# AdaLN block with attention and a mixture of low-rank experts: Strassen's scheme for the output projection of 14 groups, with the keys' rotation on VectorE ahead of the sums of the first token pair

## The chip, the cores and the metric

One core of a Trainium2 chip runs the kernel. The metric is the device time of one execution in microseconds; the time before is 2559.74 us, the median of 3 runs (2558.72 to 2560.05).

## The reference

Four batches of 512 tokens, width 1024. The part that matters here:

```
h = _layernorm(x) * (1 + ca) + sa
q = (h @ wq), k = (h @ wk), v = (h @ wv)      # 32 query heads, 8 key/value heads, 128 wide
q = _rope(q, pos); k = _rope(k, pos)
scores = q k^T * HEAD_DIM ** (-0.5)           # window of 256 keys, causal
out = softmax(scores) v                       # (tokens, 4096)
x = x + ga * (out @ wo)                       # wo is 4096 x 1024
```

An expert stage follows, which the change leaves as it is. Everything is float32.

## The kernel before

**Numbers.** Each matmul operand is split into a high and a low part (`float32r`), and `mm3` (L787) makes one product of three matmuls (lines L788 to L790). ScalarE (ACT) or GpSimd (POOL) copies the high part, VectorE (DVE) or GpSimd subtracts the low one.

**Groups.** The work is 32 groups, `n = 8 * batch + g`, one for each batch and key/value head: four query heads, one key head, one value head, and the 512 x 1024 share of the output projection that belongs to the four heads. In batch 0 the split weights are made and stored; from batch 1 on SyncE (SP) fetches them.

**One group on TensorE (PE).** `pe_attention` goes through 16 units `u` (token tile `u // 4`, head `u % 4`): scores of unit `u + 3` (L841), the turn of unit `u`'s probabilities (L859, matmul line L864), one chunk of the next group's keys in the first eight, and after every fourth unit the values of a token tile (L867). The output projection is eight halves (token tile, 512 columns) of 12 matmuls each (`pe_wo`, L816); four halves lie between the units 8 to 15 and four behind the attention. The next group's four query heads of 24 matmuls follow (`pe_project`), then its values (`pe_v`).

**Around it.** `dve_wo` (L1261) adds each half from PSUM to `acc`. `act_rope` (L1026) and `dve_rope` (L1233) rotate the keys (r = 0) and the query heads (r = 1 to 4): ScalarE copies the swapped halves, VectorE multiplies and adds, ScalarE copies the high part, VectorE subtracts the low part. `pool_group` (L766) makes the difference of the values `vd` and, for the units 8 to 15 (folded, two token tiles), multiplies a part of `pT` (L783). The values of a folded tile end with matmuls on `vd` that need these.

**SyncE's queue** runs strictly in the program's order. In a group it fetches the query and value weights when the old ones are used (`sp_fetch_qv`, L538), the keys' weights and, once the group before has projected its output, `w_o` (`sp_fetch_ko`, L545). In the first four groups of the batches 1 and 2 it also stores the next batch's normalised tile, `sp_tile_store` (L528); the tile's buffers share memory with `pT`, so ScalarE waits for this store (`s_hst`, end of `act_project`, L1082) before it goes on to the next attention. Between batches `sp_reload` (L570) loads the next batch's `hT`, which the last attention of the batch needs for its keys' chunks.

Of the kernel before, what the change touches and what calls it, by code (L numbers as in the profile page):

```python
# [19 lines left out]
F32 = mybir.dt.float32  # L20
# [34 lines left out]

def key_tiles(i):

    return list(range(max(0, i - WINDOW // P), i + 1))
# [32 lines left out]
def adaln_block(nc, x, x_turned, wq, wk, wv, wo, gate_wT, lora_aT, lora_bT, c, wmod, cos, sin, mask, keep, lower, ident, iota, out):  # L91
# [8 lines left out]
    ln_d = nc.dram_tensor("ln_scratch", (P, 2), F32, kind="Internal").ap()  # L100
    hT_d = [nc.dram_tensor(f"hT_{z}_scratch", (BATCH * P, KT, SEQ), F32, kind="Internal").ap() for z in ("hi", "lo")]

    with ExitStack() as top:
# [226 lines left out]
        def p0_pe(eng):  # L330
# [23 lines left out]
            pe_v(eng, 0, False)  # L354
# [14 lines left out]
        w_o = split_pair(p1, "w_o", [P, GQ, D])  # L369
        qo = split_pair(p1, "qo", [P, GQ, SEQ])  # L370
# [26 lines left out]
        prob = sb(p1, "prob", [P, GQ, 3 * P])  # L397
# [19 lines left out]
        with ExitStack() as a:  # L417
            lx = sb(a, "lx", [P, D])
            lf = sb(a, "lf", [P, KT, P])
            l_hi, l_lo = split_pair(a, "l", [P, KT, P])  # L420
            r_hi, r_lo = split_pair(a, "r", [P, KT, P])
        p1.close()
# [34 lines left out]
        s_dq = [sem(f"s_dq{c}") for c in range(KT // 2)]  # L457

# [74 lines left out]
        def sp_direct_group(eng, n, before_o=None):  # L533

            sp_fetch_qv(eng, n)
            sp_fetch_ko(eng, n, before_o)
# [8 lines left out]
        def sp_fetch_ko(eng, n, before_o=None):  # L545

            eng.wait_ge(s_proj, 6 * n + 2)
            if isinstance(n, int) and n == GROUPS - 1:
                eng.wait_ge(s_mm1, KT * 3)
                sp_last_rows(eng, 0)  # L550
            else:
                sp_fetch(eng, 5, (n + 1) % KV, s_dk)
            if before_o:
                before_o()
            eng.wait_ge(s_wo, 8 * n + 1)
            for j in range(6, NC):
                sp_fetch(eng, j, n % KV, s_do)
# [43 lines left out]

        def sp_groups(eng, b, rows, store):
            for t in range(QT):
                n = b * KV + 1 + t
                if not store:
                    sp_lora_load(eng, t)
                    sp_direct_group(eng, n, lambda: sp_tile_load(eng, n, rows(t)))
                else:
                    sp_turned_load(eng, b, t)
                    sp_direct_group(eng, n, lambda: sp_turned_row(eng, b, t))  # L610
                if store:
                    sp_tile_store(eng, b, t)
                else:
                    sp_lora_keep(eng, t)
            if store:
                with eng.Fori(1 + QT, KV) as g:
                    sp_direct_group(eng, b * KV + g)
            else:
                for g in range(1 + QT, KV):
                    n = b * KV + g  # L620
                    q = g - QT
                    sp_direct_group(eng, n, (lambda: sp_part(eng, q, n)) if q < 3 else None)
                    if q == 1:
                        sp_store_gate(eng, 1, part_row)
# [21 lines left out]
        def p1_sp(eng):  # L646
# [24 lines left out]
            sp_fetch_ko(eng, KV)  # L671
            for b in range(1, last):
                sp_groups(eng, b, lambda t: x_tile(b, t), True)
                sp_reload(eng, b + 1)
                sp_direct_group(eng, (b + 1) * KV)
# [75 lines left out]
        def p1_pool(eng):  # L751
# [8 lines left out]
            for b in range(1, BATCH):  # L760
                eng.wait_ge(s_fin, 2 * QT * b)
                plain(eng.memset(acc[:], 0.0)).then_inc(s_acc0, 1)
                with eng.Fori(0, KV) as g:
                    pool_group(eng, b * KV + g)

        def pool_group(eng, n):  # L766
# [6 lines left out]
            eng.wait_ge(s_fold, FOLD_STEPS * n + 2)  # L773
            eng.tensor_tensor(far[:, 0], far[:, 0], far[:, 1], ALU.add).then_inc(s_fold, 1)
            eng.wait_ge(s_fold, FOLD_STEPS * n + 3)
            plain(eng.tensor_copy(vd[:, 0], far[:, 0])).then_inc(s_fold, 1)
            eng.wait_ge(s_fold, FOLD_STEPS * n + 4)
            eng.tensor_tensor(vd[:, 1], far[:, 0], vd[:, 0].bitcast(F32), ALU.subtract).then_inc(s_fold, 1)
            for u in range(UNITS - FOLDED, UNITS):
                i, h = divmod(u, GQ)  # L780
                pair = pT_all[i % 2][:, :, :, h * P:(h + 1) * P]
                eng.wait_ge(s_ptl, UNITS * n + u + 1)
                eng.tensor_tensor(pair[:, :, 2, :], pair[:, :, 0, :].bitcast(F32), lower_t[:].unsqueeze(1).broadcast_to([P, 2, P]),  # L783
                                  ALU.mult).then_inc(s_fold, 1)
# [31 lines left out]
        def pe_wo(eng, n, half, direct):  # L816

            t, c = divmod(half, 2)
            if half == 0:
                if direct:  # L820
                    eng.wait_ge(s_do, 128 * (n - (KV - 1)))
# [4 lines left out]
            if 1 <= half < FILL:  # L826
                eng.wait_ge(s_wor, 8 * n + half + 1)
            elif half >= FILL + 3:
                eng.wait_ge(s_wor, 8 * n + half - 1)
# [9 lines left out]
        FOLD_STEPS = VD_STEPS + FOLDED  # L839
# [27 lines left out]
        def pe_values(eng, n, i):  # L867
            eng.wait_ge(s_ptl, UNITS * n + GQ * (i + 1))
            if i == 0:
                eng.wait_ge(s_v, n + 2)  # L870
            else:
                eng.wait_ge(s_ol, QT * n + i)
            kts = key_tiles(i)
            for b, kt in enumerate(kts[:prob_tiles(i)]):
                m = mm3(eng, OBANK[:], sl(v_, lambda v: v[:, kt, :]), sl(pT[i % 2], lambda p: p[:, b, :]), b == 0, b == len(kts) - 1)
            if folded(i):
                z = i - WINDOW // P
                eng.wait_ge(s_fold, FOLD_STEPS * n + VD_STEPS + GQ * (z + 1))
# [9 lines left out]
        def pe_attention(eng, n, k_at, k_direct, b1=None, o_direct=True, late=False):  # L888
            for u in range(UNITS):
# [31 lines left out]
                if u % GQ == 1 and u > GQ:  # L921
                    pe_values(eng, n, u // GQ - 1)
                if u in WO_AT:
                    pe_wo(eng, n, WO_AT.index(u), o_direct)
            pe_values(eng, n, QT - 1)
# [7 lines left out]
        def pe_qv(eng, n, direct, tile=None, part=None):  # L933
            for h in range(GQ):
                def between(k):
# [1141 lines left out]
```

## Time and profile before

| | |
|---|---|
| median of 3 runs | 2559.74 us |
| the profiled execution | 2558.81 us, span 2556.8 us |
| TensorE busy | 2532.4 us, 99% of the span |
| VectorE, ScalarE, GpSimd busy | 1609.7, 1112.4, 460.2 us |
| the 16 DMA engines | 52.5% (SyncE's queue), 197 GB/s |
| the chain that ended last | 95% on TensorE |

Busy time tells how long an engine had an instruction in it; matmuls overlap, so their starts tell the pace. The chain names the engine that the end waited for.

### The profile page before, as it was taken

What the parts mean: (1) busy time and instruction counts of PE and PEld (TensorE: products, weight loads), DVE (VectorE), ACT (ScalarE), POOL (GpSimd) and SP (SyncE); (2) the same over time, 40 slices, a digit from 0 to 9 for tenths busy, and PEclk for the clock granted to TensorE, in tenths of its full rate; (3) what the DMA queues carried; (4) which work ended last, traced back from release to release, by engine and by line L of the source; (5) the groups of instructions that cost most, each with busy time, mean ns of one, the idle gap of its engine ahead of it and who ended that gap; (6) DMA issues with size and microseconds to landing.
All of it is one profiled execution on the core that took longest, in us unless ns stands there. A gap on an engine that the chain in (4) does not pass through costs nothing.

```text
span 2556.8 us, 40925 instructions
## 1 busy us (share of the span) xinstructions
PE 2532.4 (99%) x12449; PEld 2101.0 (82%) x12449; DVE 1609.7 (63%) x4594; ACT 1112.4 (44%) x2585; POOL 460.2 (18%) x498
## 2 busy tenths in 40 slices
PE   7999999999999999999999999999999999999999
PEld 4888888887888888888888888888888888887887
DVE  6677776666666665556666665556666665556553
ACT  4555654443445443333445543333333443335441
POOL 0332233332111111102111110111111110101122
PEclk9999999999999999999999999999999999999999
DMA  8766676659445554347444554347554556446221
GB/s 339 280 222 241 246 271 224 244 179 374 171 158 190 199 183 151 117 149 298 167 167 166 197 183 164 137 148 267 189 204 175 203 201 228 180 170 261 101 83 58
DMA packets 160949, 504.15 MB, mean 197 GB/s; under 512 B 17552, under 2 KB 43984, under 8 KB 159312
## 3 DMA queue, kind: packets, MB, share of 16 engines
q1 hardware_dynamic: 156384, 486.65, 52.5%
q10 hardware_dynamic: 4464, 16.25, 1.7%
q8 instruction: 51, 0.84, 0.1%
q14 instruction: 50, 0.41, 0.0%
HBM read 381.17 MB, written 121.68 MB: 197 GB/s over the span
## 4 chain that ended last, share of the span: by engine, by line
PE 95%; DVE 2%; ACT 1%; DMA 1%; issue 1%; DVEq 0%; POOL 0%; ACTq 0%; SPq 0%; POOLq 0%
PE bank L788 30%; PE bank L790 29%; PE bank L789 29%; PE bank L864 4%; PE bank L853 1%; PE bank L1904 1%; PE bank L276 1%; PE bank L905 0%; DMA x1s<-x_scratch 0%; PE bank L303 0%; DMA wm<-in_wmod 0%; ACT w_o_hi L715 0%; PE bank L854 0%; PE bank L1955 0%; DVE qo_lo L1270 0%
## 5 line engine op out<-in xcount | busy, mean ns | idle before, releaser
L788 PE MATMUL bank<-w_o_hi,qo_hi 128*128 128x512 f32 x1024 | 411.4, 402 | 2.0 <-DVE qo_lo L1270 1.5
L790 PE MATMUL bank<-w_o_hi,qo_lo 128*128 128x512 f32 x1024 | 400.4, 391 | 0.0
L788 PE MATMUL bank<-hT_hi,w_q_hi 128*128 128x512 f32 x1024 | 399.5, 390 | 0.2 <-DVE swapped L1242 0.2
L789 PE MATMUL bank<-w_o_lo,qo_hi 128*128 128x512 f32 x1024 | 398.9, 390 | 0.0
L789 PE MATMUL bank<-hT_lo,w_q_hi 128*128 128x512 f32 x1024 | 398.5, 389 | 0.0
L790 PE MATMUL bank<-hT_hi,w_q_lo 128*128 128x512 f32 x1024 | 398.5, 389 | 0.0
L1050 ACT ACTIVATE prob<-prob,nbias 128x256 f32<-128x256 f32 (+1 forms) x512 | 247.3, 483 | 237.8 <-DVE nbias L1289 230.9
L783 POOL TENSOR_TENSOR pT<-pT,lower_t 128x256 fp32r<-128x256 f32 x256 | 196.0, 766 | 475.3 <-DVE pT L1323 475.3
L1241 DVE TENSOR_TENSOR rotated<-bank,cos_t 128x512 f32<-128x512 f32 x160 | 110.6, 692 | 261.8 <-ACT swapped L1035 261.1
L1265 DVE TENSOR_TENSOR acc<-bank,acc 128x512 f32<-128x512 f32 x256 | 173.7, 689 | 160.9 <-PE bank L790 160.8
L772 POOL TENSOR_TENSOR rotated<-v_all 128x256 f32<-128x256 f32 x64 | 48.1, 773 | 1231.5 <-DVE v_all L1329 1231.5
L1034 ACT ACTIVATE swapped<-bank 64x512 f32<-64x512 f32 x160 | 95.4, 596 | 360.4 <-PE bank L790 353.0
L1323 DVE TENSOR_TENSOR pT<-bank,pT 128x256 fp32r<-128x256 f32 (+1 forms) x512 | 195.7, 382 | 85.5 <-ACT pT L1147 85.3
L1147 ACT ACTIVATE pT<-bank 128x256 fp32r<-128x256 f32 (+1 forms) x512 | 177.5, 353 | 155.2 <-PE bank L864 150.2
L790 PEld LDWEIGHTS bank<-w_o_hi,qo_lo 128*128 128x128 f32 x1024 | 192.2, 188 | 42.2
L788 PEld LDWEIGHTS bank<-hT_hi,w_q_hi 128*128 128x128 f32 x1024 | 192.2, 188 | 42.0 <-issue 1.6
L788 PEld LDWEIGHTS bank<-w_o_hi,qo_hi 128*128 128x128 f32 x1024 | 192.3, 188 | 40.1 <-issue 3.2
L790 PEld LDWEIGHTS bank<-hT_hi,w_q_lo 128*128 128x128 f32 x1024 | 192.2, 188 | 40.0
L789 PEld LDWEIGHTS bank<-hT_lo,w_q_hi 128*128 128x128 f32 x1024 | 192.3, 188 | 39.6
L789 PEld LDWEIGHTS bank<-w_o_lo,qo_hi 128*128 128x128 f32 x1024 | 192.8, 188 | 36.7
L1289 DVE CUSTOM_DVE_ANT_0 prob<-bank,mask_t 128x256 f32<-128x256 f32 x384 | 162.4, 423 | 32.8 <-PE bank L864 10.9
L864 PE MATMUL bank<-ident_t,prob 128*128 128x128 f32 x896 | 177.1, 272 | 2.6 <-DVE prob L1299 2.1
(258 smaller groups left out, 4975.4 us busy)
## 6 DMA issues: line engine op xcount, KB each, us to landing
w_q_hi<-w_q_hi_scratch SPq DMA_DIRECT2D x96, 512.0 KB, 8.3
w_q_lo<-w_q_lo_scratch SPq DMA_DIRECT2D x96, 512.0 KB, 8.9
w_o_hi<-w_o_hi_scratch SPq DMA_DIRECT2D x96, 512.0 KB, 7.8
w_o_lo<-w_o_lo_scratch SPq DMA_DIRECT2D x96, 512.0 KB, 8.5
stage<-in_wq SPq DMA_DIRECT2D x32, 512.0 KB, 4.5
stage<-in_wo SPq DMA_DIRECT2D x32, 512.0 KB, 5.3
w_q_hi_scratch<-w_q_hi SPq DMA_DIRECT2D x32, 512.0 KB, 6.3
w_q_lo_scratch<-w_q_lo SPq DMA_DIRECT2D x32, 512.0 KB, 7.2
```

The source lines that it names most:

```text
L783: eng.tensor_tensor(pair[:, :, 2, :], pair[:, :, 0, :].bitcast(F32), lower_t[:].unsqueeze(1).broadcast_to([P, 2, P]), ALU.mult).then_inc(s ...
L788: eng.matmul(o, st[0], mv_[0], start=start, stop=False)
L789: eng.matmul(o, st[0], mv_[1], start=False, stop=False)
L790: return eng.matmul(o, st[1], mv_[0], start=False, stop=stop)
L864: m = eng.transpose(bank[5 + u % 2][:, b * P:(b + 1) * P], prob[:, u % GQ, b * P:(b + 1) * P], ident_t[:])
L1034: eng.activation(swapped[slot][0:half, :], bk[half:HD, :], ACT.Copy)
L1050: eng.activation(tile, tile, ACT.Exp, bias=nbias[:, u:u + 1], scale=-1.0, accum_out=rowsum[:, u:u + 1]).then_inc(s_exp, 1)
L1147: eng.activation(pT[i % 2][0][:, 0:nk, h * P:(h + 1) * P], bank[5 + u % 2][:, 0:nk * P].rearrange("p (b q) -> p b q", q=P), ACT.Copy).then ...
L1241: eng.tensor_tensor(rotated[slot][:], bk[:], cos_t[:], ALU.mult).then_inc(s_dve, 1)
L1265: eng.tensor_tensor(a, wo_bank(half)[:], a, ALU.add).then_inc(s_wor, 1)
L1289: plain(eng.tensor_tensor_reduce(prob[:, u % GQ, 0:w], SBANK[u % 3][:, 0:w], add, -SCALE, FAR, ALU.add, ALU.min, nbias[:, u:u + 1])).then_ ...
L1323: eng.tensor_tensor(lo, bank[5 + u % 2][:, 0:nk * P].rearrange("p (b q) -> p b q", q=P), hi.bitcast(F32), ALU.subtract).then_inc(s_ptl, 1)
```

## The change

In the batches 2 and 3 (`PAIRED = 2`) the groups but the last of each batch, 14 in all, project their output in two pairs of token tiles, (0, 1) and (2, 3). For a pair the blocks are two token tiles by two halves of the heads, times two halves of the heads by two halves of the columns, and seven products take the place of eight: `pe_product` is 6 matmuls, a pair 42, a group 84 where it had 96. The order is `ORDER = (3, 4, 1, 5, 2, 7, 6)`.

- **TensorE** runs all products behind the attention, two of them ahead of the last tile's values; the chunks of the next group's first query head take the halves' places between the units 8 to 15.
- **GpSimd** makes the five sums of attention outputs a pair (`pool_sum`) and their low parts (`pool_low`), 20 operations of 128x256 a group. The sums 1, 7 and 6 of the second pair go into the first pair's buffers and wait for its products 1, 7 and 6.
- **ScalarE** copies each tile's outputs whole (`flat_o`), the high half of them that is used plain, and the ten high parts of the sums (`act_highs`). Three of these stand between the swapped copies of the keys and their high part.
- **VectorE** adds or subtracts each product into one or two blocks of `acc`, 24 operations a group for 8 (`dve_product`), and rotates the keys after the first four.
- **The mixed weights** (five combinations of `wo` blocks a group) are made in batch 1 by GpSimd, four pieces a group for 7 groups, 28 in all, through one buffer, and stored to DRAM by SyncE: three pieces after each of the first four groups' folds, four after the others'.
- **SyncE** fetches weights one head and one product at a time in the paired groups.

```diff
+        def pool_mix(eng, piece):
+            (b11, b12), (b21, b22) = ((r[:, 0, :], r[:, 1, :]) for r in raw)
+            lo = mix_lo[:].bitcast(F32)
+            eng.wait_ge(s_raw, WS_KEPT + 32 * piece + 32)
+            eng.wait_ge(s_mixd, WS_KEPT + 32 * piece)
+            eng.tensor_tensor(lo[:, 0, :], b11, b22, ALU.add)
...
+            plain(eng.tensor_copy(mix_hi[:], lo)).then_inc(s_mix, 1)
...
+            eng.tensor_tensor(mix_lo[:], lo, mix_hi[:].bitcast(F32), ALU.subtract).then_inc(s_mix, 1)
+        def sp_mix_step(eng, at, piece, following):
+            eng.wait_ge(s_mix, 3 * at + 1)
+            if following is not None:
+                sp_mix_load(eng, following)
+            eng.wait_ge(s_mix, 3 * at + 3)
+            sp_mix_store(eng, piece)
...
+                    sp_direct_group(eng, n, b, lambda: sp_turned_row(eng, b, t))
+                    sp_mix(eng, 3 * t, [piece(3 * t + i) for i in range(4)])
+                    sp_tile_store(eng, b, t)
+                with eng.Fori(1 + QT, KV) as g:
+                    sp_direct_group(eng, b * KV + g, b)
+                    sp_mix(eng, 4 * g - 8, [piece(i, g - 2) for i in range(5)])
...
+        def pool_sum(eng, n, b, p, i):
...
+            if p == 1 and i in (1, 7, 6):
+                eng.wait_ge(s_wo, wo_at(n, b) + 1 + ORDER.index(i) + 1)
+            eng.tensor_tensor(mixed_sum(p, i)[2], x, y, op).then_inc(s_fold, 1)
...
+        M_FREE = ({7: 2, 6: 4}, {4: 6, 1: 8, 5: 10, 2: 11, 7: 12, 6: 14})
+        def pe_product(eng, n, b, p, i):
...
+            if i in M_FREE[p]:
+                eng.wait_ge(s_wor, wor_at(n, b) + 1 + M_FREE[p][i])
...
-            act_rope(eng, n, 0, False)
+            act_rope(eng, n, 0, False, (lambda: act_highs(eng, n - 1, b, ((1, 1), (1, 7), (1, 6)))) if b is not None else lambda: None)
...
         def act_groups(eng, b, ln):
+            if b == PAIRED:
+                eng.wait_ge(s_mixd, WS_KEPT + 32 * PIECES * (KV - 1))
...
+        def dve_paired_group(eng, n, b, part=None, turned=None, g=None):
+            dve_attention(eng, n - 1, b, tile=turned, paired=True)
...
+            dve_rope(eng, n, 0)
+            for i in ORDER[2:]:
+                dve_product(eng, n - 1, b, 0, i)
+            for i in ORDER:
+                dve_product(eng, n - 1, b, 1, i)
```

SyncE in a group of the first four of batch 1, from the last fetch of `w_o` on (`raw` holds the blocks of `wo`, `mix` the combinations, `l` the tile for the next batch):

```order
L569 DMA w_o_lo<-w_o_lo_scratch 128x1024
L756 DMA raw<-in_wo 128x2x256 [waits s_mix]
L756 DMA raw<-in_wo 128x2x256
L764 DMA w_s_hi_scratch<-mix_hi 640x1x256 [waits s_mix]
L764 DMA w_s_lo_scratch<-mix_lo 640x1x256
...
L592 DMA hT_hi_scratch<-l_hi 1024x1x128 [waits s_llo]
```

Before, the store of the tile followed the fetch of `w_o` directly; now three mixing steps, each like the one shown, stand between. Behind the loop of batch 1's last groups, which ends with four such steps, comes the reload of `hT`.

ScalarE at the end of a paired group's attention, up to the keys' high part:

```order
L1519 ACTIVATE flat_o<-bank 128x512 [waits s_pv]
L1520 ACTIVATE qo_hi<-bank 128x2x128
L1511 REGISTER_ALU
L1512 ACTIVATE qo_hi<-qo_sum 128x2x128 [waits s_fold]
L1403 ISA
L1408 ACTIVATE swapped<-bank 64x512 [waits s_proj]
L1409 ACTIVATE swapped<-bank 64x512
L1511 REGISTER_ALU
L1512 ACTIVATE sums_o_hi<-sums_f 128x256 [waits s_fold]
...
L1420 ACTIVATE kt_all<-rotated 128x512 [waits s_ra]
```

Three copies of `sums_o_hi` (one is shown) now lie between the swapped copies and the keys' high part; before, nothing did.

VectorE at the same place:

```order
L1650 TENSOR_TENSOR rotated<-rotated,swapped 128x512 [waits s_dve,s_rs]
L1662 TENSOR_TENSOR kt_all<-rotated,kt_all 128x512 [waits s_ra,s_rh]
L1680 REGISTER_ALU
L1684 ISA [waits s_wo]
L1686 TENSOR_TENSOR acc<-acc,bank 128x512 [waits s_wor]
```

The keys' low part, which waits for ScalarE's high part (`s_rh`), stands ahead of the 20 sums that remain; before, it stood ahead of four.

## Rows read from the trace of the kernel before

**Rows 1.** The page: busy time by engine, and the chain that ended last.
```profile
PE 2532.4 (99%) x12449; PEld 2101.0 (82%) x12449; DVE 1609.7 (63%) x4594; ACT 1112.4 (44%) x2585; POOL 460.2 (18%) x498
PE 95%; DVE 2%; ACT 1%; DMA 1%; issue 1%; DVEq 0%; POOL 0%; ACTq 0%; SPq 0%; POOLq 0%
```

**Rows 2.** TensorE's timeline, one group's last four halves: start us, us.
```profile
1323.09 0.39 PE L788 MATMUL bank<-w_o_hi,qo_hi 128*128 128x512 f32 x1
...
1333.97 0.39 PE L788 MATMUL bank<-hT_hi,w_q_hi 128*128 128x512 f32 x1
```

**Rows 3.** Groups of instructions by line: busy us, mean ns, idle before.
```profile
L783 POOL TENSOR_TENSOR pT<-pT,lower_t 128x256 fp32r<-128x256 f32 x256 | 196.0, 766 | 475.3 <-DVE pT L1323 475.3
L720 POOL TENSOR_TENSOR w_q_lo<-stage,w_q_hi 128x1024 fp32r<-128x1024 f32 x28 | 66.7, 2400 | 23.8 <-ACT w_q_hi L715 23.8
L776 POOL CAST vd<-rotated 128x256 fp32r<-128x256 f32 x32 | 12.7, 397 | 4.2
L762 POOL MEMSET acc<- 128x4096 f32 x3 | 10.6, 3529 | 79.5 <-DVE xb L1540 79.5
L1147 ACT ACTIVATE pT<-bank 128x256 fp32r<-128x256 f32 x384 | 142.6, 380 | 149.3 <-PE bank L864 144.4
L1044 ACT ACTIVATE qo_hi<-rotated 128x512 fp32r<-128x512 f32 x128 | 80.9, 632 | 210.8 <-DVE rotated L1245 210.8
L1265 DVE TENSOR_TENSOR acc<-bank,acc 128x512 f32<-128x512 f32 x256 | 173.7, 689 | 160.9 <-PE bank L790 160.8
L1257 DVE TENSOR_TENSOR qo_lo<-rotated,qo_hi 128x512 fp32r<-128x512 f32 x128 | 88.3, 690 | 55.9 <-ACT qo_hi L1044 55.9
L1434 DVE TENSOR_TENSOR stage<-stage 128x1024 f32<-128x1024 f32 x8 | 9.8, 1226 | 8.5 <-DMA stage<-ln_scratch 8.5
```

**Rows 4.** SyncE's DMA issues in batch 1, group 10: start us, us.
```profile
763.91 0.33 SPq L508 DMA_DIRECT2D w_o_hi<-w_o_hi_scratch  x1
...
767.60 0.47 SPq L508 DMA_DIRECT2D w_o_lo<-w_o_lo_scratch  x1
782.66 0.53 SPq L531 DMA_DIRECT2D hT_hi_scratch<-l_hi  x1
```

**Rows 5.** DMA of the first 20 us of that stretch, GB/s in 0.5 us slices.
```profile
GB/s 0 0 0 49 164 172 270 188 344 254 238 262 320 426 410 377 393 393 434 410 410 426 426 426 410 418 418 295 57 0 0 0 0 0 0 0 0 0 0 0
```

**Rows 6.** DMA issues of the whole run: KB each, us to landing.
```profile
hT_lo_scratch<-l_lo SPq DMA_DIRECT2D x12, 512.0 KB, 5.6
lora_b_lo_scratch<-l_lo SPq DMA_DIRECT2D x2, 512.0 KB, 3.6
```

**Rows 7.** ScalarE and TensorE where attention of that group starts.
```profile
790.54 0.40 ACT L1050 ACTIVATE prob<-prob,nbias 128x128 f32<-128x128 f32 x1 [0.47 <-DVE nbias L1289]
794.26 0.27 PE L864 MATMUL bank<-ident_t,prob 128*128 128x128 f32 x1
```

**Rows 8.** TensorE: first matmul on the folded values, attention of group 17.
```profile
1317.15 0.39 PE L788 MATMUL bank<-pT,vd 128*128 128x512 f32 x1
```

**Rows 9.** SyncE and TensorE: output weights of groups 15 and 17, keys of 16.
```profile
1119.16 0.33 SPq L508 DMA_DIRECT2D w_o_hi<-w_o_hi_scratch  x1
1152.24 0.48 PE L788 MATMUL bank<-hT_hi,w_k_hi 128*128 128x512 f32 x1
1263.11 0.33 SPq L508 DMA_DIRECT2D w_o_hi<-w_o_hi_scratch  x1
```

**Rows 10.** End of batch 1: GpSimd's last fold, SyncE's fetch, ScalarE's third exponential.
```profile
1177.60 0.73 POOL L783 TENSOR_TENSOR pT<-pT,lower_t 128x256 fp32r<-128x256 f32 x1 [0.19 <-DVE pT L1323]
1192.06 0.33 SPq L508 DMA_DIRECT2D w_o_hi<-w_o_hi_scratch  x1
1218.69 0.40 ACT L1050 ACTIVATE prob<-prob,nbias 128x128 f32<-128x128 f32 x1 [0.72 <-DVE nbias L1289]
```

**Rows 11.** GpSimd and VectorE in batch 0, two inputs from SBUF each.
```profile
121.69 2.40 POOL L720 TENSOR_TENSOR w_k_lo<-stage,w_k_hi 128x1024 fp32r<-128x1024 f32 x1 [1.61 <-ACT w_k_hi L715]
123.47 1.17 DVE L1242 TENSOR_TENSOR swapped<-swapped,sin_t 128x512 f32<-128x512 f32 x1
```

More of the change, by code:

```diff
@@ new lines, in sp_mix_load, with sp_mix_store @@
+        def sp_mix_load(eng, piece):
+            g, jc = (piece[0], piece[1])
+            j, half = divmod(jc, 2)
+            for y in range(2):
+                rows = wo[bass.ds(g * GQ * HD + (j + 2 * y) * HD, HD), :].rearrange("p (c s n) -> p c s n", c=2, s=2)[:, :, half, :]
+                eng.dma_start(raw[y][:], rows).then_inc(s_raw, 16)
+        def sp_mix_store(eng, piece):
+            g, jc = piece
+            j, half = divmod(jc, 2)
+            for z, tile in enumerate((mix_hi, mix_lo)):
+                to = w_s[z][bass.ds(g * P, P), :].rearrange("p (i j s n) -> p i j s n", i=len(MIXED), j=2, s=2)[:, :, j, half, :]
+                eng.dma_start(to, tile[:].bitcast(F32)).then_inc(s_mixd, 16)
@@ L611, in sp_groups @@
[L611 to L624, printed above, removed]
+                    sp_paired_group(eng, n, b, False, lambda: sp_tile_load(eng, n, rows(t)), lambda: sp_lora_keep(eng, t))
@@ L626, in x_tile @@
+            for g in range(1 + QT, KV):
+                n = b * KV + g
+                q = g - QT
+                sp_paired_group(eng, n, b, g == KV - 1, (lambda: sp_part(eng, q, n)) if not store and q < 3 else lambda: None)
+                if not store and q == 1:
+                    sp_store_gate(eng, 1, part_row)
         def x_tile(b, t):
@@ L759, in p1_pool @@
             pool_group(eng, KV - 1)
-            for b in range(1, BATCH):
+            eng.wait_ge(s_fin, 2 * QT)
+            plain(eng.memset(acc[:], 0.0)).then_inc(s_acc0, 1)
+            with eng.Fori(1, 1 + QT) as g:
+                pool_group(eng, KV + g - 1)
+                for i in range(3):
+                    pool_mix(eng, 3 * g - 3 + i)
+            with eng.Fori(1 + QT, KV + 1) as g:
+                pool_group(eng, KV + g - 1)
+                for i in range(4):
+                    pool_mix(eng, 4 * g - 8 + i)
@@ L1023, in adaln_block, with pe_group, act_rope @@
+        def pe_group(eng, n, b, direct, tile=None):
+            pe_attention(eng, n - 1, b, K_AT, direct, o_direct=direct)
+            for half in range(FILL, 8):
+                pe_wo(eng, n - 1, b, half, direct)
+            pe_qv(eng, n, direct, b, tile)
         OUT_STEP = {GQ * i + GQ + 1 + LAG: i for i in range(QT - 1)}
-        def act_rope(eng, n, r, split, between=lambda: None):
+        def act_rope(eng, n, r, split, between=lambda: None, b=None):
             slot = r % 2
```

584 lines of the change are left out of this document (452 added, 132 removed).

## The prediction

> **What bounds the kernel now.** I read the page first: TensorE has an instruction in it for 99% of the span, and 95% of the chain that ended last lies on it [rows 1]. So a matmul removed is time removed, as long as no new wait takes its place, and a wait put before TensorE costs its full length. The pace comes from the timeline: the 48 matmuls of four halves take 1333.97 - 1323.09 = 10.88 us, 0.227 us each [rows 2]. The next views tell what lies beside TensorE: GpSimd is the idlest engine (18%) but slow per element [rows 3], SyncE's queue runs in order [rows 4], and ScalarE's first work of an attention stands close behind the tile's store [rows 7].
>
> **The change, part by part.** The sum is made against the profiled execution, 2558.8 us, 0.9 us below the median of the runs.
>
> *Fewer matmuls.* 12 of 96 go in each of 14 groups: 12 x 0.227 = 2.7 us a group, **-38 us**. The first query head's chunks between the units cost what they cost behind the attention.
>
> *The keys' rotation ahead of the sums.* On VectorE the keys' low part waits for ScalarE's high part; that copy now stands behind three copies of sums, the last of which needs GpSimd's sum 6 of the second pair, and this one needs TensorE's product 6 of the first pair to be done. TensorE meanwhile has one product to run, the second pair's 3 (6 x 0.227 = 1.4 us); the next, 4, needs the bank of product 1, which VectorE has left standing behind the keys. The chain: end of the matmul behind its successor's start 0.16 (0.39 less 0.227) [rows 2], GpSimd's sum 0.77, ScalarE's copies 0.38 and 0.63, VectorE's low part 0.69, two sums, 0.6 and 0.69 [rows 3], six handings-over at some 0.06 (an estimate): 4.3 us. Less 1.4 that is 2.9 us a group. GpSimd can still hold it: in batch 0 a VectorE operation with two SBUF inputs took 1.17 us and ended 0.55 us after GpSimd's, where its median is 0.68 [rows 11]. The keys' low part is such an operation and GpSimd then makes low parts. I add 0.4: 3.3 us x 14 = **+46 us**. Bounds: 2.5 (the three engines overlap more) to 4 us (GpSimd half an operation late twice), 35 to 56 us. The Trainium skill, "SBUF — State Buffer", section on the two separate sides, says that VectorE with two SBUF inputs and GpSimd share one port pair and the loser is fully blocked; the rows agree. By that rule the wait is 3.3 us, without it 2.9, some 6 us over 14 groups.
>
> *VectorE's 16 further sums* are 16 x 0.6 = 9.6 us a group. They end some 3 us behind the last product, and one query head of 24 matmuls (5.4 us) covers this in a plain group. In the four groups of batch 2 that also normalise a tile, two operations of 1.23 us [rows 3] and ScalarE's eight pieces follow in the same chain, and TensorE waits for a bank: 1.8 us at the last head and about 1 at the first turn, 2.9 us x 4 = 12, and about 1 us in each of the four groups that split the experts' weights: **+16 us**, bounds 0 and 30.
>
> *The pieces of mixed weights in batch 1.* A piece on GpSimd is five sums of 256 columns (5 x 0.75), a cast of 1280 and a subtraction of 1280. 1024 columns of subtraction took 2.40 us, so 3.0; a cast of 256 took 0.40 and 4096 columns of memset 3.5, so about 1.3 [rows 3]. Together 8.1 us. One buffer holds it, so the next piece waits for the store, 1.31 MB in two DMAs. Pairs of 0.52 MB took 5.6 + 0.6 us (runs of 512 bytes) and 3.6 + 0.4 us (4 KB) from the first issue to the last landing [rows 6]; with 2 us fixed and the rest in proportion that is 4.5 to 7.3, and I take 6, since the runs are 1 KB. A piece's cycle is then 14.3 us with 0.2 of waits.
>
> - *Groups 9 to 12, three pieces.* Take group 10, where the fetch of `w_o` is issued at 763.9 [rows 4]. GpSimd made its first piece long before, but SyncE can only now store it: issued at 769, behind 4.2 MB that occupy the engines to about 777 [rows 5]; 0.52 MB of `raw` and the store land at 782. Second piece to 790.2, landed 796.4, third to 804.6. Only then does SyncE issue the store of the tile, at 782.7 before [rows 4]: with 2.4 MB in line, landed at 814.5. ScalarE waits for this store before the attention; its third exponential ran at 790.5, TensorE's turn of that unit at 794.3 [rows 7]. From the release to the turn are 1.7 us of work: 816.3. That is 22 us, four times: **+88 us**. Low end: no line behind `w_o` and the shortest stores, tile landed at 801, 8.4 us; high end 26 us; 34 to 104.
> - *Attentions 13 and 14, four pieces.* Counted from the fetch of `w_o`, the fourth piece ends at 18.1 + 8.1 + 2 x 14.3 + 0.2 = 55 us. Then the values' difference (3.7, five operations) and four folds (3.1) are still to do: 62 us. TensorE wanted them at 1317.15 - 1263.11 = 54.0 [rows 8, 9]. **+16 us** for both, 0 to 28.
> - *Attention 15.* SyncE reloads `hT` only behind the fourth piece's store: 1119.2 + 55 = 1174.2, first pair landed 8.9 us later (2 fixed, 4.1 for the store, 2.6 for 1.05 MB at 410 GB/s, 0.2). The keys' chunk that needs it ran at 1152.2 [rows 9]. **+31 us**, 19 to 36.
> - *Attention 16.* ScalarE waits for all 28 stores. GpSimd is free at 1178.3 [rows 10]; the pieces end at 1187, 1202, 1218 and 1232, the second and third also held by the weights fetched from 1192.1 on [rows 10]; the last store has 4.2 MB ahead, landed 1240.6. The exponential ran at 1218.7 [rows 10]; after the same correction of 2 us **+20 us**, 8 to 25.
>
> Batch 1 gives 88 + 16 + 31 + 20 = 155 us, the paired groups -38 + 46 + 16 = +24. The sum is 2558.8 + 179 = **2738 us**, slower. With all low ends it is 2617, with all high ends 2800.
>
> **What stays free.** The weights' fetches of the paired groups have most of a group each (71 us) to land, and the DMA engines are little over half used. The sums on GpSimd in the attention: 16 operations of 0.8 us lie between the values' low part and the last fold, some 17 us with the waits, against a need on TensorE about 20 us after it; if they were 3 us slower, the last tile's values would wait. VectorE in the attention loses four sums to `acc` and gains nothing; its steps of about 1.4 us lie under TensorE's.
>
> **The rivals.**
> 1. *Some of batch 1 is hidden.* The stores land earlier than the order of issue says and a piece is quicker. With all four at their low ends and the rest as summed: 2558.8 + 24 + 61 = 2644. For it: 410 GB/s are reached in the queue [rows 5]. Against: two pieces alone are 16 us, and the tile's store had only 1.2 us of room between its landing (issue of the second DMA some 0.6 us behind 782.66, and 5.6: 788.8) and ScalarE's wait.
> 2. *The mixing costs nothing.* The paired groups alone decide: 2583, slower still. It would take the tile's store issued by 784, two pieces and two stores within 20 us of the fetch of `w_o`: not possible with pieces of 8 us [rows 3].
> 3. *Faster: TensorE's shorter run shows.* Mechanism: GpSimd finishes its pieces before anyone asks, and the keys' chain is covered by the second pair's product 3. Place: TensorE between products 3 and 4. It decides once that chain falls under 1.4 us and the waits of batch 1 under 38 us together; the price is -38: 2521. Against it: five operations of known length stand in the chain.
> 4. *GpSimd and VectorE block each other in batch 1 too.* Subtractions of 3.0 us hold rotations, and these hold pieces. The pieces then take 10 us: 2 us more in each of the 2 to 3 pieces that stand in each of the waits, some 16 + 12 + 6 + 6 = 40 us: 2778, and up to 2800.
>
> That the change does not do what it says can be left out: the order shows 84 matmuls for 96 in the paired groups.
>
> **How the numbers follow.** The sum as it stands (2680 to 2765) has 0.58; rival 4 (2765 to 2800) 0.13; rival 1 (2600 to 2680) 0.14; rival 2 (2562 to 2600) 0.07; faster 0.06; no change 0.02. The range 2635 to 2785 takes the first whole, most of rival 4 and most of rival 1, about 0.8. A difference of 0.2% (5 us) is about what a measurement of this kernel can tell from none. Faster 0.06, same 0.02, slower 0.92.
>
> **What would show it.** In the profile after: ScalarE idle for about 22 us before an exponential or a copy of `pT`, released by the DMA into the scratch of `hT`, four times; TensorE idle about 31 us before the keys' chunk of attention 15, released by a load of `hT`; 14 waits of 2.5 to 4 us before the second pair's product 4, released by VectorE's sums; pieces about 14 us apart on GpSimd. The prediction is wrong if the tile's store lands before ScalarE asks for it, if pieces follow each other in 9 us, or if TensorE goes from product 3 to 4 without a wait.

## The result, and the profile after

The changed kernel takes 2813.47 us (median of 4 runs, 2810.20 to 2816.11) against 2559.45 us before in the same comparison: 1.099 times the time, 95% interval 1.097 to 1.101. That is slower by 254 us, where 2738 us and 179 us were forecast, and above the range's end of 2785 us.

The page of the changed kernel, the rows that answer to [rows 1], and the granted clock of TensorE in 40 slices of the span (tenths of full speed, all 9 before):

```profile
PE 2555.4 (91%) x12281; PEld 2097.1 (75%) x12281; DVE 1817.4 (65%) x4818; ACT 1166.0 (41%) x2781; POOL 892.4 (32%) x974
PEclk9999999999889889997989999999999999999999
PE 63%; issue 11%; POOL 8%; DMA 7%; DVE 6%; ACT 3%; SPq 2%; DVEq 0%; POOLq 0%; ACTq 0%
```

TensorE's busy time is 23 us longer although it has 168 matmuls fewer, since some of them ran at half the clock, and it now stands idle for 9% of the span. GpSimd's busy time has nearly doubled (460.2 to 892.4 us). The chain that ended last lies on TensorE for 63% where it was 95%; GpSimd and DMA, which hardly stood in it before, have 15% together, and 11% is "issue", time in which nothing that the profile shows was waited for.

The view of waits, TensorE's rows (us in total, times, longest):

```profile
PE bank L1243 <- DVE prob L1727: 143.6, 29, 26.3
PE bank L1079 <- DVE acc L1686: 38.2, 14, 3.0
PE bank L1079 <- DMA hT_lo<-hT_lo_scratch: 29.9, 1, 29.9
PE bank L1079 <- DVE acc L1670: 9.3, 8, 1.9
PE bank L1079 <- POOL pT L1074: 8.6, 2, 4.3
```

The second row is the forecast chain of the keys. The first mixes four waits of 18.5 to 18.8 us for the tile's store, one of 26.3 at the entry into batch 2, and smaller ones. The last is the wait for GpSimd's folds in attentions 13 and 14.

TensorE's timeline, the first matmul of each group's values, of the changed kernel, groups 9 to 17 but for 12 (start us, us); between two such rows lies the first one's attention:

```profile
716.49 0.45 PE L1079 MATMUL bank<-hT_hi,w_v_hi 128*128 128x512 f32 x1
815.34 0.45 PE L1079 MATMUL bank<-hT_hi,w_v_hi 128*128 128x512 f32 x1
914.04 0.45 PE L1079 MATMUL bank<-hT_hi,w_v_hi 128*128 128x512 f32 x1
...
1110.43 0.45 PE L1079 MATMUL bank<-hT_hi,w_v_hi 128*128 128x512 f32 x1
1193.04 0.45 PE L1079 MATMUL bank<-hT_hi,w_v_hi 128*128 128x512 f32 x1
1274.00 0.45 PE L1079 MATMUL bank<-hT_hi,w_v_hi 128*128 128x512 f32 x1
1384.53 0.45 PE L1079 MATMUL bank<-hT_hi,w_v_hi 128*128 128x512 f32 x1
1488.15 0.50 PE L1079 MATMUL bank<-hT_hi,w_v_hi 128*128 128x512 f32 x1 [0.43 <-DVE swapped L1647]
```

and of the kernel before, groups 9 and 10:

```profile
714.83 0.45 PE L788 MATMUL bank<-hT_hi,w_v_hi 128*128 128x512 f32 x1
785.89 0.45 PE L788 MATMUL bank<-hT_hi,w_v_hi 128*128 128x512 f32 x1
```

One such row to the next is a group: 71.06 us before. After, the stretches that hold attentions 9 to 12 take 393.94 us together, 109.7 more than four of before; attentions 13 and 14 cost 21.5 more, attention 15 takes 110.53 where it took 72.90 (37.6 more), and attention 16 costs 32.6. Ahead of the first row 1.7 us are lost, and from the last to the end another 52.

**The store of the tile.** SyncE's queue in group 10 (the first row is the fetch of the output weights, the last two the tile's store):

```profile
793.37 0.33 SPq L569 DMA_DIRECT2D w_o_hi<-w_o_hi_scratch  x1
...
821.98 0.59 SPq L764 DMA_DIRECT2D w_s_hi_scratch<-mix_hi  x1
822.61 0.65 SPq L764 DMA_DIRECT2D w_s_lo_scratch<-mix_lo  x1
...
836.05 0.65 SPq L764 DMA_DIRECT2D w_s_lo_scratch<-mix_lo  x1
836.75 1.37 SPq L592 DMA_DIRECT2D hT_hi_scratch<-l_hi  x1
838.16 1.48 SPq L592 DMA_DIRECT2D hT_lo_scratch<-l_lo  x1
```

and what waited for it, on ScalarE and TensorE:

```profile
845.94 0.40 ACT L1426 ACTIVATE prob<-prob,nbias 128x128 f32<-128x128 f32 x1 [22.77 <-DMA hT_lo_scratch<-l_lo]
847.17 0.47 PE L1243 MATMUL bank<-ident_t,prob 128*128 128x128 f32 x1 [18.60 <-DVE prob L1727]
```

The store is issued 43.4 us behind the fetch; the forecast had 40.7. ScalarE stands 22.8 us, TensorE 18.6.

**VectorE is held.** GpSimd, VectorE and TensorE in the same group:

```profile
818.61 3.35 POOL L980 TENSOR_TENSOR mix_lo<-mix_lo,mix_hi 128x1280 fp32r<-128x1280 f32 x1
819.22 3.29 DVE L1650 TENSOR_TENSOR rotated<-rotated,swapped 128x512 f32<-128x512 f32 x1
823.53 0.33 PE L1243 MATMUL bank<-ident_t,prob 128*128 128x128 f32 x1 [2.90 <-DVE prob L1727]
```

An addition that took 0.69 us before takes 3.29 us, and ends 0.55 us behind GpSimd's subtraction, as in [rows 11]. TensorE waits 2.9 us for what follows. From 644 to 1488 us 36 operations of 512 columns with two inputs from SBUF on VectorE (additions, subtractions and multiplications) take over 0.75 us, together 33 us more than at 0.69 each; in the kernel before, the same groups have none.

**Half the clock after a wait.** TensorE's timeline at the second pair's product 4, behind attention 20:

```profile
1762.32 0.70 PE L1079 MATMUL bank<-w_o_hi,qo_hi 128*128 128x512 f32 x1 [2.68 <-DVE acc L1686]
1762.81 0.63 PE L1080 MATMUL bank<-w_o_lo,qo_hi 128*128 128x512 f32 x1
1763.24 0.63 PE L1081 MATMUL bank<-w_o_hi,qo_lo 128*128 128x512 f32 x1
...
1766.07 0.40 PE L1079 MATMUL bank<-w_o_hi,sums_o_hi 128*128 128x512 f32 x1
1766.30 0.40 PE L1080 MATMUL bank<-w_o_lo,sums_o_hi 128*128 128x512 f32 x1
```

and the view of stretches there: us, busy (instructions), granted clock, DMA share, GB/s:

```profile
1758.50:1762.30 3.80, 1.14 (x6) 1.00 0.41 113
1762.30:1765.80 3.50, 3.48 (x9) 0.52 0.43 177
1766.00:1770.00 4.00, 4.00 (x19) 1.00 0.97 311
```

While TensorE waited the clock was still at 1.00; behind the wait it is 0.52, that is 1.2 GHz instead of 2.4, for 3.5 us, and matmuls follow each other in 0.43 us instead of 0.227. The nine from 1762.32 to 1766.07 take 3.75 us for 2.04: 1.7 us beyond the wait. Ten of the 14 waits for the keys (2.68 to 2.96 us) were followed by such a stretch; four (2.68 to 2.77 us) were not. In the waits of 18 us and more the clock fell within the wait.

**GpSimd holds the keys' low part as well.** GpSimd and VectorE just ahead of that product:

```profile
1759.09 1.42 POOL L1015 TENSOR_TENSOR sums_o_lo<-sums_f,sums_o_hi 128x256 fp32r<-128x256 f32 x2
1760.14 0.93 DVE L1662 TENSOR_TENSOR kt_all<-rotated,kt_all 128x512 fp32r<-128x512 f32 x1 [3.49 <-ACT kt_all L1420]
```

The keys' low part took 0.91 to 0.93 us beside the products of all 14 paired groups, and 0.69 at the change from batch 2 to 3, where there are none.

**VectorE stands without a releaser.** At the start of attention 21, on VectorE and TensorE:

```profile
1797.07 0.29 DVE L1715 TENSOR_TENSOR prob<-bank,mask_t 128x128 f32<-128x128 f32 x1 [2.50 <-issue]
1801.00 0.29 DVE L1717 CUSTOM_DVE_ANT_0 prob<-bank,prob 128x128 f32<-128x128 f32 x1 [3.64 <-issue]
1801.82 0.48 PE L1243 MATMUL bank<-ident_t,prob 128*128 128x128 f32 x1 [4.34 <-DVE prob L1727]
```

VectorE's program has jumped back to the start of a loop (groups 21 to 23) some 6 us before the first stall begins. The same happens in attention 22. The loop over groups 17 to 20 jumps back too, and in its attentions no stall without a releaser is over 1.3 us.

### The profile page after: what moved, and what is told of

Its sections match the earlier page's. It is cut to its first block, busy times and chain, and to the rows that moved or that the text cites. A ratio compares the mean times of both kernels' runs of the same rounds, so it can differ in the third digit from the quotient of the medians.

```text
span 2812.1 us, 42764 instructions
## 1 busy us (share of the span) xinstructions
PE 2555.4 (91%) x12281; PEld 2097.1 (75%) x12281; DVE 1817.4 (65%) x4818; ACT 1166.0 (41%) x2781; POOL 892.4 (32%) x974
## 4 chain that ended last, share of the span: by engine, by line
PE 63%; issue 11%; POOL 8%; DMA 7%; DVE 6%; ACT 3%; SPq 2%; DVEq 0%; POOLq 0%; ACTq 0%
PE bank L1079 19%; PE bank L1081 19%; PE bank L1080 19%; DMA raw<-in_wo 3%; PE bank L1243 3%; POOL mix_lo L980 2%; DMA hT_lo_scratch<-l_lo 1%; SPq L569 1%; DVE acc L1686 1%; POOL mix_hi L978 1%; DVE swapped L1647 1%; DVE rotated L1650 1%; POOL sums_f L1009 1%; POOL mix_lo L973 1%; POOL mix_lo L976 1%
## 5 line engine op out<-in xcount | busy, mean ns | idle before, releaser
L1080 PE MATMUL bank<-hT_lo,w_q_hi 128*128 128x512 f32 x912 | 355.5, 390 | 0.0
L1079 PE MATMUL bank<-w_o_hi,qo_hi 128*128 128x512 f32 x744 | 302.6, 407 | 49.6 <-DVE acc L1686 38.2
L1081 PE MATMUL bank<-w_o_hi,qo_lo 128*128 128x512 f32 x744 | 294.4, 396 | 0.0
L1080 PE MATMUL bank<-w_o_lo,qo_hi 128*128 128x512 f32 x744 | 293.0, 394 | 0.0
L1243 PEld LDWEIGHTS bank<-ident_t,prob 128*128 128x128 f32 x896 | 122.8, 142 | 184.0 <-DVE prob L1727 162.1
L1420 ACT ACTIVATE qo_hi<-rotated 128x512 fp32r<-128x512 f32 x128 | 80.8, 631 | 406.2 <-DVE rotated L1650 406.1
L1686 DVE TENSOR_TENSOR acc<-acc,bank 128x512 f32<-128x512 f32 x336 | 205.3, 677 | 10.4 <-PE bank L1081 8.9
L1079 PEld LDWEIGHTS bank<-w_o_hi,qo_hi 128*128 128x128 f32 x744 | 141.2, 190 | 87.6 <-DVE acc L1686 34.6
L1079 PE MATMUL bank<-hT_hi,w_k_hi 128*128 128x512 f32 x368 | 169.3, 460 | 30.5 <-DMA hT_lo<-hT_lo_scratch 29.9
L1727 DVE TENSOR_SCALAR prob<-prob,rrow 128x256 f32<-128x256 f32 (+1 forms) x512 | 194.0, 384 | 0.2 <-issue 0.2
```

Of the source, the lines that this page charges most:

```text
L1079: eng.matmul(o, st[0], mv_[0], start=start, stop=False)
L1080: eng.matmul(o, st[0], mv_[1], start=False, stop=False)
L1081: return eng.matmul(o, st[1], mv_[0], start=False, stop=stop)
L1243: m = eng.transpose(bank[5 + u % 2][:, b * P:(b + 1) * P], prob[:, u % GQ, b * P:(b + 1) * P], ident_t[:])
L1420: eng.activation(dst, rotated[slot][:], ACT.Copy).then_inc(s_rh, 1)
L1686: eng.tensor_tensor(a, a, M_BANK[p][i][:], ALU.add if sign > 0 else ALU.subtract).then_inc(s_wor, 1)
```

## The experiments

**The tile's store.** It was moved from the third step to behind the first.

```diff
-                    sp_mix(eng, 3 * t, [piece(3 * t + i) for i in range(4)])
+                    sp_mix(eng, 3 * t, pieces[:2])
                     sp_tile_store(eng, b, t)
+                    sp_mix(eng, 3 * t + 1, pieces[1:])
```

> The changed kernel with the store of the tile moved from behind the third mixing step to behind the first, in the first four groups of batch 1; nothing else. Theory 1 (SyncE's order holds ScalarE): the four waits of 18.7 us before a turn of probabilities go, and with them the 1.5 us that TensorE runs at half its clock after each; against that the load of the next tile still stands behind the third step, 46 us after the first fetch of the output weights, and its statistics on VectorE are now wanted at about 41 us: a new wait of about 10 us in three of the groups. 2813 - 80 + 30 = 2763 us. Theory 2 (the stores are late because the pieces and the DMA engines are slow, wherever they stand): the tile lands no more than 5 us earlier, 2790 us or more.

Measured: 2744.55 us (1.073 of before, 1.072 to 1.075), 69 us less. SyncE's and TensorE's timelines, group 10:

```profile
777.76 0.33 SPq L569 DMA_DIRECT2D w_o_hi<-w_o_hi_scratch  x1
...
796.54 0.52 SPq L592 DMA_DIRECT2D hT_hi_scratch<-l_hi  x1
797.10 0.68 SPq L592 DMA_DIRECT2D hT_lo_scratch<-l_lo  x1
807.93 0.48 PE L1245 MATMUL bank<-ident_t,prob 128*128 128x128 f32 x1 [2.87 <-DVE prob L1729]
```

The store is issued 18.8 us behind the fetch, as before the change, and the wait of 18.6 us is gone. At the statistics, where a new wait of 10 us was expected, VectorE stands 2.8 us for the tile's load and TensorE behind it 0.5 us. The wait of 2.9 us stays, since the pieces still run there. Theory 1 holds for the mechanism; its price for what comes next was too high.

**The keys' rotation.** On VectorE it was moved behind the sums of the first pair.

```diff
-            dve_rope(eng, n, 0)
             for i in ORDER[2:]:
                 dve_product(eng, n - 1, b, 0, i)
+            dve_rope(eng, n, 0)
```

> The changed kernel with the rotation of the keys on VectorE moved behind the five remaining products' sums of the first token pair. Theory 1: the 14 waits of 2.7 us before the second pair's product 4 go (38 us), and with them the stretches of 4 us at half clock that follow some nine of them (1.8 us each, 16 us): 2813 - 54 = 2759 us. Theory 2 (the wait only moves): VectorE is then late with the sums of the second pair, TensorE waits some 2 us before product 7 or 6, and the time falls by no more than 15 us, 2798 us or more.

Measured: 2778.07 us (1.086, 1.084 to 1.088), 35 us less. The waits for `acc` L1686 (38.2 us) have no row any more; two others have grown:

```profile
PE bank L1243 <- DVE prob L1727: 147.2, 29, 25.0
PE bank L1079 <- DVE swapped L1647: 10.5, 7, 2.1
```

by 3.6 and 7.1 us over the changed kernel. So the place of the rotation costs 35 us, between the two theories. Of the waits and of the half clock behind ten of them, 38 + 17 us, a third comes back; 7.1 us of it are seen at the query heads that follow, where VectorE is now late.

**The length of GpSimd's instruction.** Its subtraction of 1280 columns was cut into five of 256.

```diff
-            eng.tensor_tensor(mix_lo[:], lo, mix_hi[:].bitcast(F32), ALU.subtract).then_inc(s_mix, 1)
+            for i in range(len(MIXED)):
+                ins = eng.tensor_tensor(mix_lo[:, i, :], lo[:, i, :], mix_hi[:, i, :].bitcast(F32), ALU.subtract)
+            ins.then_inc(s_mix, 1)
```

> The changed kernel with GpSimd's low part of a mixed piece made by five subtractions of 256 columns instead of one of 1280. Theory 1 (VectorE operations with two inputs from SBUF are held while one of GpSimd's runs): no VectorE operation of 512 columns lasts over 1.6 us where now some last 3.3, TensorE's waits of 2.9 us before the second turn in groups 9 to 12 fall below 1 us and the half clock after them goes (4.4 us less in each of four groups, some 2 us in three more); a piece is 0.7 us longer, which costs 1.4 us in each of four groups and 2 to 3 us in the others: 2813 - 24 + 14 = 2803 us. Theory 2 (the engines do not hold each other, VectorE is late for another reason): the 3.3 us stay, and the longer pieces cost 14 us, 2827 us.

Measured: 2818.92 us (1.102, 1.100 to 1.104), 5 us more. No operation of 512 columns on VectorE lasts over 1.62 us, and the waits of 2.9 us in attentions 10 to 12 are 1.0 to 1.2: the hold lasts as long as GpSimd's single instruction. But 51 operations are held instead of 36, and they hold GpSimd in turn: the five took 3.4 us alone and 4.4 us beside VectorE. Each piece in SyncE's order lengthens the wait for the tile, by 3.8 us in group 10:

```profile
848.09 0.48 PE L1245 MATMUL bank<-ident_t,prob 128*128 128x128 f32 x1 [22.36 <-DVE prob L1729]
```

The waits for GpSimd's folds in attentions 13 and 14 grow from 4.3 us to 9.3 and 8.2. Cutting the instruction is no remedy while somebody waits for the sum of the pieces.

**All moved.** Four pieces behind the folds of each of seven attentions, and SyncE's steps spread over the group: the first ahead of the fetch of the output weights, the tile's store behind the second, the fourth behind the next query weights.

```diff
+        def sp_slot_group(eng, n, b, s, row=None, store=None, earlier=True):
+            sp_fetch_qv(eng, n)
...
+                sp_slot_step(eng, s, 0)
+            sp_fetch_ko(eng, n, b, before_o, (lambda: sp_slot_step(eng, s - 1, 3)) if earlier else None)
+            sp_slot_step(eng, s, 1)
+            if store:
+                store()
+            sp_slot_step(eng, s, 2)
```

> The changed kernel with all of it moved: four pieces after each of the folds of batch 1's first seven attentions (none is left for the entry into batch 2), the first step of a group ahead of the fetch of the output weights, the fourth behind the next fetch of the query weights, the tile's store behind the second step, the high part stored ahead of the low one, the low part in five subtractions, and the keys' rotation behind the first pair's sums. Theory 1 (order in the queues, held VectorE and the keys' chain make all of the loss): batch 1 is back at 71 us a group give or take 2, the paired groups at 68.5 to 71: 2559.5 - 38 + 12 for stalls of VectorE with no releaser + 10 for late ropes = 2545 us. Theory 2 (the pieces cost something wherever they stand, by held VectorE operations or DMA load): batch 1 keeps 5 us or more in each group, 2580 us or more.

Measured: 2614.65 us (1.022, 1.020 to 1.023), 199 us less than the change. The time is that of theory 2: the groups with a tile still take 77.7 to 78.4 us. The next two of batch 1 take 73 and 75, so the 5 us that it gave to each group are not in all of them.

**What a wait costs.** In the kernel before, TensorE was made to wait in the groups whose output weights are fetched, in a second kernel for longer by four operations on VectorE whose output nobody reads.

```diff
+            elif half == FILL + 1 and direct:
+                eng.wait_ge(s_wor, 8 * n + half + 1)
```

> The kernel before, with TensorE held in each of the 24 groups whose output weights are fetched: it starts the second of the last four halves only when VectorE has added the first. The wait is the end of a matmul, one addition of 0.69 us and the handings-over, about 1.0 us. Theory 1 (a wait costs its length, and from about 2.5 us on TensorE then also runs for some 4 us at 1.2 GHz): a wait of 1.0 us is too short for that, 24 x 1.0 = 24 us, 2583 us, granted clock 1.0. Theory 2 (any wait brings the half clock): 24 x 2.8 = 67 us, 2626 us.

> The same, with four further VectorE operations of 376 columns ahead of that addition, which write to a tile that nobody reads: the wait becomes about 3.1 us. Theory 1: 24 x 3.1 = 74 us, and 1.8 us at half clock after each, 43 us: 2676 us, granted clock below 0.98. Theory 2 (the half clock in the changed kernel came from something else than the wait, so that here a wait costs its length): 2633 us, granted clock 1.0.

Measured: 2695.05 us (1.053, 1.051 to 1.055) and 2734.56 us (1.068, 1.067 to 1.070). The waits in the two, the shorter and the longer:

```profile
PE bank L788 <- DVE acc L1267: 84.3, 24, 5.2
```

```profile
PE bank L789 <- DVE acc L1273: 126.8, 25, 7.0
```

Each sum has one wait of 0.5 us that the kernel before has as well, and the second has one of 1.5 us in batch 0. That leaves 23 waits of 3.2 to 5.2 us (83.7 together) and 23 of 5.0 to 7.0 us (124.8). The first kernel's was meant to be 1.0 us, but the keys' rotation stands ahead of that addition on VectorE: my misreading of the order. The time above before is 136.0 and 175.5 us. Beyond the waits (in the second the one in batch 0 too) 52.3 and 49.2 us remain, **some 2.2 us for each of 23 waits** (2.3 and 2.1), whether it lasted 3.6 or 5.4 us on average. The granted clock of the whole run is 0.979 and 0.972, and a stretch at half goes with each of the 23.

So theory 1 of the second kernel holds: the half clock comes with the wait alone. The first can't tell its own two theories apart, since no wait in it was short enough. For shorter ones there are the traces of the other kernels: in the changed kernel none of the 13 waits of 1.0 to 2.3 us (from 644 us on) was followed by half clock; in the complete version below, waits of 1.5 us were.

**GpSimd with one input.** The five sums and the low part were replaced by copies (so the mixed weights are no combinations).

```diff
-            eng.tensor_tensor(lo[:, 0, :], b11, b22, ALU.add)
...
+            for i, block in enumerate((b11, b12, b21, b22, b11)):
+                ins = plain(eng.tensor_copy(lo[:, i, :], block))
```

> The changed kernel with GpSimd's mixed pieces made by copies in place of the five sums and the low part (the mixed weights are then no combinations, and the attention's output is not the reference's): each of GpSimd's operations there has one input from SBUF instead of two. A piece is shorter with it, some 4.6 us for 8.1. Theory 1 (two operations with two SBUF inputs, one on each engine, hold each other): no VectorE operation of 512 columns lasts over 0.9 us in batch 1 outside the folds, and the waits of 1.9 and 2.9 us in groups 9 to 12 are gone, in addition to what the shorter pieces save (two in the tile's wait, three to four in the others): 2813 - 66 - 29 = 2718 us. Theory 2 (any work of GpSimd holds VectorE): operations of 1 us and more stay, and waits of 1 us or more with them; 2813 - 66 = 2747 us.

Measured: 2742.51 us (1.071, 1.070 to 1.073), nearer to theory 2. The waits of 1.9 and 2.9 us are gone, and attentions 13 and 14 cost nothing (71.4 and 71.2 us). But 22 of VectorE's operations are still over 0.75 us (7.6 us too much together, the longest 1.74), and 21 of them lie beside GpSimd's copies and casts. So GpSimd needs no second input to hold VectorE; the copies are only shorter. One such pair, GpSimd's cast and VectorE's multiplication:

```profile
807.53 1.26 POOL L978 CAST mix_lo<-mix_hi 128x1280 fp32r<-128x1280 f32 x1
808.24 1.09 DVE L1645 TENSOR_TENSOR swapped<-swapped,sin_t 128x512 f32<-128x512 f32 x1
```

The tile's wait is 16.1 us, 2.5 less than 18.6, where two pieces shorter by 3.5 us each let 7 be expected.

**Without mixing.** No pieces, loads or stores in batch 1; the paired groups fetch plain weights in stretches of the same size.

```diff
-                for i in range(3):
-                    pool_mix(eng, 3 * g - 3 + i)
...
-                if i in MIXED:
-                    at = MIXED.index(i) * D
-                    kept_o = w_s[z][bass.ds(g * P, P), at:at + D].rearrange("p (j n) -> p j n", j=2)
```

> The changed kernel without the mixing in batch 1 (no pieces, no loads, no stores, no wait for them); the paired groups fetch stretches of the plain output weights of the same size instead of the mixed ones, so the output is not the reference's. Theory 1 (all that the groups 9 to 17 lose is the mixing's): the groups of batch 1 are back at 71.05 us, the paired groups as in the changed kernel, 2813 - 204 = 2609 us; the scheme alone is then 50 us slower than before, by the keys' wait with its half clock (14 x 4.5 less what some groups are spared) and waits of late VectorE. Theory 2 (some of it belongs to the paired groups' entry or to the moved fetches): 2620 us or more.

Measured: 2616.98 us (1.023, 1.021 to 1.024). Mixing costs 196.5 us of the 254, and the rest of the scheme loses 58. The groups of batch 1 take 71.05 to 71.15 us. In batch 1 no operation on VectorE of 512 columns is over 0.75 us. TensorE's waits, and ScalarE at the start of attention 29:

```profile
PE bank L1066 <- DVE acc L1671: 38.2, 14, 3.0
PE bank L1230 <- DVE prob L1712: 24.2, 16, 5.8
PE bank L1066 <- DVE swapped L1632: 5.6, 7, 1.4
2205.47 0.40 ACT L1413 ACTIVATE prob<-prob,nbias 128x128 f32<-128x128 f32 x1 [8.42 <-DMA mod_scratch<-lf]
```

The last row is a wait that I had not foreseen: ScalarE stands 8.4 us for SyncE's store of the late gate, which stands behind a fetch of mixed weights that waits for TensorE.

**The floor of the scheme.** The same kernel with the keys' rotation moved and VectorE's loop over groups 21 to 23 written out; in a second one that store of the gate as well goes ahead of the wait for TensorE.

```diff
-                    with eng.Fori(1 + QT, KV) as g:
+                    for g in range(1 + QT, KV):
                         dve_paired_group(eng, b * KV + g, b)
...
                 sp_head(eng, 3, (n + 1) % KV)
+                before_last()
                 eng.wait_ge(s_proj, 6 * n + 7)
                 sp_mixed(eng, 3, g)
```

> The kernel without mixing, with the keys' rotation behind the first pair's sums, and with VectorE's loop over the last three paired groups of batch 2 written out (the same instructions, no jump back). Theory 1 (in those groups VectorE stands for up to 6 us at the loop's start without any releaser, since it jumps back there): written out, the stalls of 2.5 and 3.6 us go, and groups 22 and 23 fall from 75 to 77 us to below 71: with the 35 us that the keys' move gave alone, 2617 - 35 - 12 = 2570 us. Theory 2 (the stall is not the jump's): 2582 us. In both cases the scheme without its mixing stays slower than before.

> The same, with SyncE's store of the late gate in batch 3 ahead of the wait for the values' projection instead of behind it. Theory 1 (ScalarE stands 6 us before the third exponential of group 30 because that store is issued late): group 30 loses the wait of 5.7 us and the half clock after it, 6 to 7 us less than the run before: 2563 us. Theory 2 (the gate itself is ready late): no change.

Measured: 2563.74 us (1.0019, 1.0009 to 1.0028) and 2553.75 us (0.9978, 0.9968 to 0.9987). Both theories 1 hold, the first as far as writing the loop out removes the stalls; why they stand there isn't shown by it. The stretches of attentions 21 and 22 fall from 78.7 and 79.1 to 68.6 us, 2.5 below before, by the keys' move and the loop together. The loop without the keys' move is seen between the two complete versions, where these two fall by 14 us. No stall on VectorE without a releaser is over 1.3 us in the batches 1 to 3. The stretch of attention 29 falls from 81.7 to 73.0 us with the gate's store. So with its mixing for nothing and three mends the scheme gains 5 us of the 38 that the matmuls promise.

**The best complete version.** All moved, with the loop written out and the gate's store earlier.

> The kernel with all moved (2614.7 us), with VectorE's loop written out and the gate's store earlier: 2615 - 13 - 6 = 2596 us if both theories hold, still slower than before, since GpSimd's pieces of two inputs from SBUF lengthen VectorE's operations in batch 1 wherever they stand; 2615 us if neither does.

Measured: 2588.03 us (1.0115, 1.0098 to 1.0132), 225 us less than the change and still 29 more than before. Its largest waits in total:

```profile
PE bank L1247 <- DVE prob L1731: 25.6, 19, 3.0
PE bank L1083 <- DVE swapped L1651: 8.6, 6, 2.1
PE bank L1236 <- DVE qo_lo L1666: 5.4, 9, 1.5
```

Against the floor of 2553.75 us the mixing still costs 34 us, although no engine on TensorE's path waits for a store of the tile or of the pieces. What the trace shows for it in batch 1 are VectorE operations over 0.75 us (73, 30 us too much together), waits of 3.0, 2.9, 2.8 and 1.5 us before turns in attentions 9 to 12 with half clock behind each, and one of 2.2 us for the load of `hT`; its share by cause was not measured. None of the experiments points to a version that beats the kernel before, so none was made.

## Why the prediction was wrong

The direction and the places that it named were right; the sum was 75 us short, 41 in batch 1 and 34 in the paired groups. Three steps failed. The clock had no term at all. The term for VectorE's further sums, +16, stands against 54 measured. The terms of batch 1, +155 against 196.5, took each wait for a store or a fold, and neither the held operations of VectorE nor the half clock behind the waits. Step by step:

- **Fewer matmuls**, -38: a plain paired group without other waits takes 68.6 us where it took 71.05, so -34. Right but for 4 us.
- **The keys' chain**, +46: 14 waits of 2.7 to 3.0 us, 38.2 in all, by the chain as described. GpSimd did hold the keys' low part, as assumed, but by 0.24 us (0.93 for 0.69) and not 0.4, and even so the wait was below the 2.9 of the estimate without a hold. What the step left out of the hold is batch 1, where rotations for the first turns of an attention stand beside the pieces' longer instructions. The Trainium skill, "SBUF — State Buffer", section on the two separate sides, says that whichever starts first has the shared ports for its whole instruction; the 3.29 us beside GpSimd's 3.35 agree. The step also left out the clock: ten of the waits brought 1.6 to 1.8 us more.
- **VectorE's further sums**, +16: without mixing the scheme loses 58 us. Against -34 and 38.2 that leaves 54, the largest error of one term. The half clock behind six of the keys' waits in that kernel is some 10, VectorE's stalls without a releaser some 14 (75.96 + 75.07 us against 68.58 + 68.59 in the two complete versions), the gate's store 9, and none of them was in the sum. By subtraction some 21 are left for the kind that was forecast, late query heads and first turns.
- **Groups 9 to 12**, +88, measured 109.7. With attention 10 the 27.6 us are waits of 18.6 for the store (22 forecast), 2.9 and 1.9 behind held operations of VectorE, and 4.2 that remain, about what its two stretches of half clock would cost. The store's part was right within 3.4 us, the pieces following each other in 15.1 to 15.3 us for 14.3; the other two parts were not there.
- **Attentions 13 and 14**, +16, measured 21.5, and by another mixture: the wait for GpSimd's folds, forecast at 8 us each, was 4.3 each, and the rest is waits of 1.1 to 2.3 us behind VectorE and half clock. That this total came near is luck. **Attention 15**, +31, measured 37.6 with a wait of 29.9. **Attention 16**, +20, measured 32.6, of which 4.6 belong to the paired group and not to the mixing; its wait is 26.3, six more than reckoned.

The common fault is that each wait was priced at its own length. The trace of before could not show more: its granted clock is 1.00 throughout, and from group 8 on TensorE never waits over 0.7 us. Bounds from the nearest rows should then have said that nothing is known above them. Rival 4, that the engines hold each other in batch 1 too, was true as a mechanism but priced as longer pieces; what the traces show is its effect on VectorE's own chain. Rivals 1 to 3 fell: no store was hidden, TensorE waited at every place named, and without the mixing the time is 2617, where rival 2 had 2583.

## What to carry to other kernels

Before a queue that runs in order is given a step that waits for a slow engine, look for what stands behind it and who waits for that: moving one store two steps forward gave 69 us here. Each wait on TensorE of 3 us or more that was measured here cost its length and about 2 us more, so a saving of 2.7 us a group is spent by the first such wait that it creates. And work for an idle GpSimd is not free where VectorE's critical chain has operations with two inputs from SBUF beside it: price each by GpSimd's longest single instruction there.

## What the hardware did that was not expected

- Behind waits of 2.7 to 30 us the granted clock of TensorE was at half for 2.9 to 6.5 us, where it fell at all. The cost was 2.3 and 2.1 us a wait in the two kernels that measured it alone, whatever the wait's length. Waits of 2.68 us were followed by it in some groups and not in others. So were shorter ones: of 1.95 us in the kernel with the tile's store moved, and of 1.48 and 1.50 us in the best complete version. What decides is open.
- A VectorE operation of a single column with two inputs (128x1, `lnv`) took 2.6 us beside a GpSimd subtraction of 1280 columns, for 0.16 us before, so the hold does not ask for a large operation.
- VectorE stood for 2.5 and 3.6 us in each of the two attentions behind a jump back in one loop; with that loop's body written out the stalls were gone. The other loop over paired groups jumps back as well and shows none, so a jump alone isn't enough; what VectorE stood for stays open.
